# Softplus of the scans' preparation: summed in PSUM by identity matmuls instead of on VectorE

## The chip, the cores and the metric

The kernel runs on one core of a Trainium2 chip. The metric is the device time of one execution in microseconds (us). The engines are PE (TensorE), DVE (VectorE), ACT (ScalarE), POOL (GpSimd) and SP (SyncE, which only issues transfers).

## The reference, cut to what matters

The input is (8, 56, 56, 128) in f32: 8 images of 3136 pixels. Layers 0, 2 and 3 are deformable convolutions (each output pixel gathers 36 points, with bilinear weights, followed by a small MLP). Layer 1 is a two-dimensional state-space layer: over each image run four scans (rows, columns, both reversed) of 256 channels with 16 states each.

```python
x_dbl = jnp.einsum('bkdl,kcd->bkcl', xs, x_proj_w)
dts, Bsm, Csm = jnp.split(x_dbl, [R, R + N], axis=2)
dt = jnp.einsum('bkrl,kdr->bkdl', dts, dt_projs_w)
dt = jax.nn.softplus(dt + dt_projs_b[None, :, :, None])
...
def step(h, t):
    dt_t, u_t, B_t, C_t = t
    h = h * jnp.exp(dt_t[..., None] * A) + (dt_t * u_t)[..., None] * B_t[:, :, None, :]
    y = jnp.einsum('bkdn,bkn->bkd', h, C_t)
    return (h, y)
```

The change touches the line with `softplus` and the product `dt_t * u_t` behind it.

## The kernel before, in words

**Stages.** The deformable layers make 24 stages (3 layers x 8 images), in the order of `stage_order` (line 53), numbered 0 to 23; stage 20 is layer 2 of image 6, stage 21 layer 3 of image 6, stages 22 and 23 are layers 2 and 3 of image 7. A stage writes its projected image as a table to HBM, computes indices and weights in groups of four tiles of 128 pixels ("pr", DVE line 1724 writes the indices), and gathers. The gathers are indirect DMAs that POOL issues one by one (line 909). Twelve of them make a "third" of a tile, in one of five slots `d_g`. DVE multiplies a third by its weights (line 1523, "weigh"), PE sums it into PSUM by identity matmuls (line 1197, "sum"), which frees the slot for POOL (semaphore `accq`).

**Scans.** The state-space layer of an image runs beside the gathers of other images. It has 28 pieces (4 directions x 7 chunks of 448 pixels) of 16 states each, so 448 scan steps per image and 3584 in all. A step is: PE spreads B and C into banks `l_pb` and `l_pc` (line 1152), DVE multiplies dt*u by B (line 1497), ACT makes exp(dt*A) for both channel halves (line 961), DVE scans half 0 at once (line 1476) and half 1 in two parts (lines 1479 and 1482), multiplies by C (line 1503), ACT saves the carry (line 940), and PE adds the product to `l_acc` (line 1183).

**The preparation of a piece ("h", 224 times, nine parts 0 to 8)** runs one piece ahead. Part 0 projects into bank `r[1]` (`d_pr1`, called r1 here). Parts 1 and 2 put dt's projection for one channel half each into r1, from where ACT takes |x| into `e` (line 991) and relu(x) into `dtu` (line 994), which frees r1. Then, all on SBUF tiles of 128 x 896: exp(-|x|) on ACT (line 1000), u = 1 + e on DVE (1546), the rounding error (u - 1) - e on DVE (1549), relu minus that error on DVE (1553), ln u on ACT (1003), the sum dt on DVE (1557), and dt*u by the pixels on DVE (1561 for rows, 1563 for columns).

**What sets the order.** `Planner` puts scan ticks and stage work into one list; `takes_r1` tells it which scan items use bank r1, which the stages' own fetches ("ax"), tables ("at"), convolutions ("ac") and indices ("pr") share. The uses of a bank are numbered in that list's order. `schedule` looks for the pace, the number of scan ticks per third. `interleave` then makes each engine's own fixed queue out of lanes. All engines run their queues in order.

## Time and profile before

| | us |
|---|---|
| median of 3 runs | 28853.25 (28846.84 to 28859.32) |
| the profiled execution: device time | 28895.68 |
| the profiled execution: span, first to last instruction | 28893.9 |
| busy: PE / DVE / POOL / ACT | 22353.6 / 22852.5 / 21557.8 / 12154.5 |
| mean granted TensorE clock | 0.866 of 2.4 GHz |

A span is counted between the first and last recorded instruction. "Busy" leaves out the issuing and waiting of an engine's sequencer. The idle time named with a group is that of the engine just before its instructions, with what ended it; "issue" is time in which the engine waited for nothing that the profile shows.

### The profile page before, as it was taken

Reading aid. Unit: us, or ns where it says so; the run is one execution under the profiler, and the core shown is the slowest. Engines: PE = TensorE matmul, PEld = TensorE weight load, DVE = VectorE, ACT = ScalarE, POOL = GpSimd, SP = SyncE. Lnnn points to the kernel's source line nnn. Section 1 sums busy time; section 2 is a strip of 40 time slices with the busy share of each in tenths; the row PEclk is TensorE's granted clock in tenths of the full one; section 3 lists DMA queues with packets and bytes.
Section 4 is the critical chain, followed back from the end, with each engine's and each line's share of the span. In section 5 each row is a group of like instructions: output and inputs, shape, how many; then the busy total and the mean of one; then the engine's idle time right before and its main releaser. Section 6 shows DMA issues by size and latency. Waiting matters only on the chain.

```text
span 28893.9 us, 291528 instructions
## 1 busy us (share of the span) xinstructions
PE 22353.6 (77%) x94224; PEld 14447.1 (50%) x94224; DVE 22852.5 (79%) x36206; ACT 12154.5 (42%) x21719; POOL 21557.8 (75%) x21172
## 2 busy tenths in 40 slices
PE   6588788787887888877888788778878787777544
PEld 4455455454554555545545455445545454445443
DVE  2399988999699979998799969997899969995221
ACT  1254445444444445444444444444444444443100
POOL 6777777777777777777777777777777777576767
PEclk7798899898998999888998889889988898888666
DMA  3222132221322222212222132212222222112221
GB/s 79 69 59 69 54 77 65 59 69 54 79 66 56 68 69 64 69 54 67 71 65 69 54 78 60 62 56 75 66 62 63 56 76 58 47 53 73 65 57 53
DMA packets 2410696, 1854.82 MB, mean 64 GB/s; under 512 B 1686547, under 2 KB 2045509, under 8 KB 2409165
## 3 DMA queue, kind: packets, MB, share of 16 engines
q0 software_dynamic: 677376, 1388.62, 17.1%
q1 hardware_dynamic: 1731788, 447.55, 6.9%
q8 instruction: 746, 12.22, 0.2%
q14 instruction: 786, 6.43, 0.1%
HBM read 1569.35 MB, written 265.21 MB: 63 GB/s over the span
## 4 chain that ended last, share of the span: by engine, by line
POOL 63%; issue 21%; PE 7%; DVE 6%; ACT 1%; DMA 1%; SPq 1%; DVEq 0%; POOLq 0%; ACTq 0%
POOL d_g L909 63%; PE d_p L1197 2%; DVE l_wk L1476 1%; DVE l_wk L1497 1%; DVE l_wk L1503 1%; PE l_acc L1183 1%; PE d_pr L1347 1%; DVE d_g L1523 1%; DVE l_wk L1479 1%; PE l_pc L1312 0%; SPq L805 0%; DMA l_wk<-mid 0%; PE d_pr L1336 0%; PE d_pr L1335 0%; DMA d_g<-table,d_idx 0%
## 5 line engine op out<-in xcount | busy, mean ns | idle before, releaser
L909 POOL DMA_INDIRECT d_g<-table,d_idx x21168 | 21557.6, 1018 | 7300.2 <-issue 6436.2
L1197 PE MATMUL d_p<-d_g,c_ident 128*128 128x128 f32 x43200 | 6734.4, 327 | 2711.1 <-DVE d_g L1523 2709.5
L1197 PEld LDWEIGHTS d_p<-d_g,c_ident 128*128 128x128 f32 x43200 | 6503.2, 240 | 3408.7 <-DVE d_g L1523 2926.5
L1183 PE MATMUL l_acc<-l_wk,c_ident 128*128 128x448 f32 x14336 | 6597.3, 585 | 114.2 <-DVE l_yx L1461 102.1
L961 ACT ACTIVATE l_pm<-l_wk,l_a 128x448 f32<-128x448 f32 x3584 | 2282.6, 637 | 8608.2 <-DVE l_wk L1476 8585.1
L1503 DVE TENSOR_TENSOR l_wk<-l_wk,l_pc 128x896 f32<-128x896 f32 x3584 | 3857.3, 1076 | 493.2 <-PE l_pc L1152 254.2
L1497 DVE TENSOR_TENSOR l_wk<-l_wk,l_pb 128x896 f32<-128x896 f32 x3584 | 3836.5, 1070 | 85.9 <-PE l_pb L1152 83.4
L1183 PEld LDWEIGHTS l_acc<-l_wk,c_ident 128*128 128x128 f32 x14336 | 2921.8, 205 | 1827.8 <-issue 1725.8
L1476 DVE TENSOR_TENSOR_SCAN l_wk<-l_pm,l_carry,l_wk 128x448 f32<-128x448 f32 x3072 | 3522.9, 1147 | 1.0
L1523 DVE TENSOR_TENSOR d_g<-d_g,d_wt 128x512 f32<-128x512 f32 (+1 forms) x1385 | 880.4, 690 | 2559.7 <-DMA d_g<-table,d_idx 2559.5
L1523 DVE TENSOR_TENSOR d_g<-d_g,l_pm 128x1536 f32<-128x1536 f32 (+1 forms) x1309 | 2279.8, 1742 | 429.2 <-DMA d_g<-table,d_idx 379.6
L1152 PE MATMUL l_pc<-l_spl,c_sel 96*128 96x448 bf16 x3584 | 1356.0, 378 | 1501.1 <-DVE l_wk L1503 1494.7
L1482 DVE TENSOR_TENSOR_SCAN l_wk<-l_wk 128x224 f32<-128x224 f32 x3584 | 2448.3, 683 | 1.5
L961 ACT ACTIVATE l_wk<-l_wk,l_a 128x448 f32<-128x448 f32 x3584 | 2339.5, 653 | 2.9 <-DVE l_wk L1557 0.9
L1152 PE MATMUL l_pb<-l_spl,c_sel 96*128 96x448 bf16 x3584 | 1334.9, 372 | 1191.9 <-DVE l_wk L1497 1184.5
L1479 DVE TENSOR_TENSOR_SCAN l_wk<-l_wk,l_carry 128x224 f32<-128x224 f32 x3072 | 2051.0, 668 | 1.0
L1152 PEld LDWEIGHTS l_pb<-l_spl,c_sel 96*128 96x128 bf16 x3584 | 354.6, 99 | 2684.6 <-DVE l_wk L1497 2267.7
L1152 PEld LDWEIGHTS l_pc<-l_spl,c_sel 96*128 96x128 bf16 x3584 | 361.7, 101 | 2387.5 <-DVE l_wk L1503 2130.7
L961 ACT ACT_TABLE_LOAD x1132 | 1452.4, 1283 | 126.9 <-DVE l_wk L1476 107.9
L1347 PE MATMUL d_pr<-d_xt,d_diag 128*128 128x448 f32 x3024 | 1270.6, 563 | 23.7 <-ACT d_xt L1076 17.8
L1112 ACT ACTIVATE d_ys<-d_p 128x256 f32<-128x256 f32 x288 | 109.0, 378 | 2434.8 <-PE d_p L1197 2430.2
L1770 DVE BATCH_NORM_STATS2 d_bs<-d_pr 128x6 f32<-128x128 f32 (+1 forms) x1200 | 297.7, 289 | 887.0 <-PE d_pr L1403 492.0
(180 smaller groups left out, 24483.5 us busy)
## 6 DMA issues: line engine op xcount, KB each, us to landing
d_g<-table,d_idx POOLq DMA_INDIRECT x21168
table<-d_pst SPq DMA_DIRECT2D x2376, 64.0 KB
hd<-d_hst SPq DMA_DIRECT2D x168, 224.0 KB
d_htc<-hd SPq DMA_DIRECT2D x144, 256.0 KB
d_xin<-mid SPq DMA_DIRECT2D x112, 224.0 KB, 2.9
mid<-d_xo SPq DMA_DIRECT2D x192, 128.0 KB
d_xres<-mid SPq DMA_DIRECT2D x192, 128.0 KB
d_xin<-in_x SPq DMA_DIRECT2D x56, 224.0 KB, 3.2
```

Of the source, the lines that this page charges most:

```text
L909: e.indirect_dma_start(out=m.g[Q % SLOTS][:, j, :], out_offset=None, in_=m.table[k % 2], in_offset=bass.IndirectOffsetOnAxis(ap=m.idx[G % ...
L961: e.activation(m.dA0 if h == 0 else m.dA1[x % 3], m.dt[P % 2][:, h, :], ACT.Exp, scale=m.aa[:, kd, h, n:n + 1]).then_inc(s[f"dA{h}"], 1)
L1152: return e.matmul(bank[:, 0:448], m.sel[:, row + n:row + n + 1].to_broadcast([96, 128]), m.spl[P % 2][:, :], start=True, stop=True)
L1183: ins = e.matmul(m.acc[:, h, 0:448], m.ident[:, :], m.hb[x % 4][:, h, :], start=(n == 0), stop=(n == 15))
L1197: ins = e.matmul(m.p0[:, t % 2 * 128:t % 2 * 128 + 32 * w], m.ident[:, :], m.g[Q % SLOTS][:, w * p:w * p + w, 32 * r:32 * r + 32], start=( ...
L1347: ins = e.matmul(m.r[1][:, 0:448], m.diag[:, j, :], m.xt[:, 8 * c + dy:8 * c + dy + 8, dx:dx + 56], start=(j == 0), stop=(j == 8))
L1476: e.tensor_tensor_scan(hb[:, 0, way], m.dA0[:, way], hb[:, 0, way], ini, ALU.mult, ALU.add).then_inc(s["sh"], 1)
L1479: e.tensor_tensor_scan(hb[:, 1, one], dA1[:, one], hb[:, 1, one], ini, ALU.mult, ALU.add).then_inc(s["s1h"], 1)
L1482: e.tensor_tensor_scan(hb[:, 1, two], dA1[:, two], hb[:, 1, two], hb[:, 1, mid:mid + 1], ALU.mult, ALU.add).then_inc(s["sh"], 1)
L1497: e.tensor_tensor(m.hb[x % 4][:, :, :], m.dtu[P % 2][:, :, :], bc(m.pb[:, 0:448], 1, 2), ALU.mult).then_inc(s["f_pb"], 1)
L1503: e.tensor_tensor(m.hb[x % 4][:, :, :], m.hb[x % 4][:, :, :], bc(m.pc[:, 0:448], 1, 2), ALU.mult).then_inc(s["f_pc"], 1)
L1523: ins = e.tensor_tensor(g, g, wt, ALU.mult)
```

## The change

The softplus is computed from the same terms, elsewhere. Per channel half: after |x| and relu(x), ACT writes exp(-|x|) back into bank r1 (which is therefore not free yet) and copies -u = -(1 + e) from there into `dt`. DVE forms the rounding correction from -u (SBUF) and e (PSUM) into `e` in one instruction of 448 columns, and frees the bank. ACT takes ln over both halves at once, as before. PE adds relu, ln and the correction in r1 by three identity matmuls; ACT copies the sum to `dt`; DVE multiplies the sum, from PSUM, by the pixels and frees the bank. Five of nine parts use r1 now.

```diff
 def takes_r1(item):
-    return item[0] == "c" or item[0] == "h" and item[3] < 3
+    return item[0] == "c" or item[0] == "h" and item[3] < 5
...
# ACT
-                e.activation(m.dtu[P % 2][:, h, :], m.r[1][:, 0:448], ACT.Relu, bias=bia).then_inc(s["f_r1"], 1)
+                e.activation(m.dtu[P % 2][:, h, :], m.r[1][:, 0:448], ACT.Relu, bias=bia).then_inc(s["ab"], 1)
+                e.wait_ge(s["ab"], 4 * P + 2 * h + 2)
+                e.activation(m.r[1][:, 0:448], m.e[:, h, :], ACT.Exp, scale=-1.0).then_inc(s["ex"], 1)
+                e.wait_ge(s["ex"], 2 * P + h + 1)
+                e.activation(m.dt[P % 2][:, h, :], m.r[1][:, 0:448], ACT.Copy, scale=-1.0, bias=-1.0).then_inc(s["uu"], 1)
...
-                e.activation(m.e[:, :, :], m.e[:, :, :], ACT.Exp, scale=-1.0).then_inc(s["ex"], 1)
-            elif st == 6:
-                e.wait_ge(s["qq"], P + 1)
-                e.activation(m.dt[P % 2][:, :, :], m.dt[P % 2][:, :, :], ACT.Ln).then_inc(s["ln"], 1)
+                e.wait_ge(s["f_r1"], J.free("h1", P))
+                e.activation(m.dt[P % 2][:, :, :], m.dt[P % 2][:, :, :], ACT.Ln, scale=-1.0).then_inc(s["ln"], 1)
+            elif st in (4, 5):
+                h = st - 4
+                e.wait_ge(s["p_r1"], J.full(f"s{h}", P))
+                e.activation(m.dt[P % 2][:, h, :], m.r[1][:, 0:448], ACT.Copy).then_inc(s["d1"], 1)
...
# PE
+            elif st in (3, 4):
+                h = st - 3
+                e.wait_ge(s["ln"], P + 1)
+                e.wait_ge(s["f_r1"], J.use[f"s{h}", P])
+                e.matmul(m.r[1][:, 0:448], m.ident[:, :], m.dtu[P % 2][:, h, :], start=True, stop=False)
+                e.matmul(m.r[1][:, 0:448], m.ident[:, :], m.dt[P % 2][:, h, :], start=False, stop=False)
+                e.matmul(m.r[1][:, 0:448], m.ident[:, :], m.e[:, h, :], start=False, stop=True).then_inc(s["p_r1"], 1)
...
# DVE
-                e.tensor_scalar(dt[:, :, :], m.e[:, :, :], 1.0, None, ALU.add).then_inc(s["uu"], 1)
...
-                e.scalar_tensor_tensor(m.e[:, :, :], dt[:, :, :], -1.0, m.e[:, :, :], ALU.add,
-                                       ALU.subtract).then_inc(s["qq"], 1)
...
-                e.tensor_tensor(dtu[:, :, :], dtu[:, :, :], m.e[:, :, :], ALU.subtract).then_inc(s["s1"], 1)
...
-                e.tensor_tensor(dt[:, :, :], dtu[:, :, :], dt[:, :, :], ALU.add).then_inc(s["d1"], 1)
...
-                    e.tensor_tensor(dtu[:, :, :], dt[:, :, :], m.pixels(m.xb[:, :, :], kd, c), ALU.mult).then_inc(s["d2"], 1)
...
+            elif st in (3, 4):
+                h = st - 3
+                e.wait_ge(s["uu"], 2 * P + h + 1)
+                e.scalar_tensor_tensor(m.e[:, h, :], dt[:, h, :], 1.0, m.r[1][:, 0:448], ALU.add,
+                                       ALU.add).then_inc(s["f_r1"], 1)
+            elif st in (5, 6):
+                h = st - 5
+                e.wait_ge(s["d1"], 2 * P + h + 1)
+                z, to = m.r[1][:, 0:448], dtu[:, h, :]
+                if kd % 2:
+                    z, to = (x.rearrange("p (x y) -> p x y", y=56) for x in (z, to))
+                e.tensor_tensor(to, z, m.pixels(m.xb[:, h, :], kd, c), ALU.mult).then_inc(s["f_r1"], 1)
```

In the kernel after, DVE's correction is line 1559 and its product line 1567; the scan's lines 1476, 1479, 1482, 1497, 1503 and 1523 are 1490, 1493, 1496, 1511, 1517 and 1537; PE's spreads, product sums and gather sums (1152, 1183, 1197) are 1159, 1190 and 1204; the identity matmuls are lines 1234 to 1236. The order calls scans SCALAR_TENSOR_TENSOR.

DVE, preparation of piece 51 (image 1, columns reversed), before. `l_wk0` is e, `l_wk4` is dtu, `l_wk2` is dt:

```order
L1546 TENSOR_SCALAR l_wk2<-l_wk0 128x896
L1482 SCALAR_TENSOR_TENSOR l_wk9<-l_wk5,l_wk9 128x224
L1549 SCALAR_TENSOR_TENSOR l_wk0<-l_wk2,l_wk0 128x896
L1503 TENSOR_TENSOR l_wk8<-l_wk8,l_pc 128x896
L1553 TENSOR_TENSOR l_wk4<-l_wk4,l_wk0 128x896
L1696 TENSOR_TENSOR d_cc<-d_pr1,c_hw 128x288
L1697 TENSOR_REDUCE d_mx<-d_pr1 128x16
L1557 TENSOR_TENSOR l_wk2<-l_wk4,l_wk2 128x896
L1700 TENSOR_TENSOR d_ee<-d_pr1,d_mx 128x144
L1702 TENSOR_SCALAR d_cc<-d_cc 128x288
L1563 TENSOR_TENSOR l_wk4<-l_wk2,l_xb 128x896
```

DVE, the same piece in the changed kernel, from its second correction to its first product (`d_pr1` is bank r1):

```order
L1559 SCALAR_TENSOR_TENSOR l_wk0<-l_wk2,d_pr1 128x448
L1490 SCALAR_TENSOR_TENSOR l_wk10<-l_pm,l_carry,l_wk10 128x448
L1493 SCALAR_TENSOR_TENSOR l_wk10<-l_wk5,l_carry,l_wk10 128x224
L1511 TENSOR_TENSOR l_wk11<-l_wk3,l_pb 128x896
L1496 SCALAR_TENSOR_TENSOR l_wk10<-l_wk5,l_wk10 128x224
L1517 TENSOR_TENSOR l_wk9<-l_wk9,l_pc 128x896
L1490 SCALAR_TENSOR_TENSOR l_wk11<-l_pm,l_carry,l_wk11 128x448
L1493 SCALAR_TENSOR_TENSOR l_wk11<-l_wk6,l_carry,l_wk11 128x224
L1511 TENSOR_TENSOR l_wk8<-l_wk3,l_pb 128x896
L1496 SCALAR_TENSOR_TENSOR l_wk11<-l_wk6,l_wk11 128x224
L1517 TENSOR_TENSOR l_wk10<-l_wk10,l_pc 128x896
L1567 TENSOR_TENSOR l_wk4<-d_pr1,l_xb 128x448
```

The chain stood within one scan step; now it is spread over several, and the instructions left are half as wide and read the bank.

PE, the first sum of the same piece in the changed kernel:

```order
L1159 MATMUL l_pb<-l_spl0,c_sel 128x448
L1234 MATMUL d_pr1<-l_wk4,c_ident 128x448
L1235 MATMUL d_pr1<-l_wk2,c_ident 128x448
L1236 MATMUL d_pr1<-l_wk0,c_ident 128x448
L1159 MATMUL l_pc<-l_spl0,c_sel 128x448
L1190 MATMUL l_acc<-l_wk9,c_ident 128x448 x2
```

The three matmuls stand between the spread of B and the spread of C; before, nothing of the softplus was in PE's queue.

Counted over the whole queues: ACT has 3193 table loads before and 3215 now; copies of weights to PSUM (line 968), each of which lets a third be weighed in one instruction instead of three, are 1309 before and 1227 now. On DVE, between the last weighing of a stage and the last part of the next one's first index group stand 50 scan steps before at the change from stage 20 to 21, and 39 now; at the other changes that part stands ahead of the last weighing or at most one step behind it, before and now. By the end of stage 20 DVE's queue has 3386 of the 3584 steps before and 3441 now. An image's scans had ended and the next one's not begun at the change from stage 16 to 17 before (image 5), and now at those from 5 to 6 (image 1) and 13 to 14 (image 4).

## Rows read from the trace of the kernel before

**Rows 1.** The page: busy time by engine, and POOL's group of gathers
```profile
PE 22353.6 (77%) x94224; PEld 14447.1 (50%) x94224; DVE 22852.5 (79%) x36206; ACT 12154.5 (42%) x21719; POOL 21557.8 (75%) x21172
...
L909 POOL DMA_INDIRECT d_g<-table,d_idx x21168 | 21557.6, 1018 | 7300.2 <-issue 6436.2 <-DVE d_idx L1724 504.7 <-PE d_p L1197 270.4
```
**Rows 2.** The waits of POOL: us in total, times, longest
```profile
POOL d_g L909 <- DVE d_idx L1724: 504.7, 4, 259.5
POOL d_g L909 <- PE d_p L1197: 270.4, 43, 34.4
```
**Rows 3.** Line 909 by window: length, busy (instructions), clock, DMA share, GB/s
```profile
1262.00:25060.00 23798.00, 18126.81 (x17640) 0.90 0.24 65
26549.00:28894.00 2345.00, 1683.06 (x1764) 0.64 0.21 59
```
**Rows 4.** Timeline, 6633 to 6640 us, DVE and POOL: start, length
```profile
6633.34 1.08 DVE L1503 TENSOR_TENSOR l_wk<-l_wk,l_pc 128x896 f32<-128x896 f32 x1
...
6636.14 1.08 DVE L1557 TENSOR_TENSOR l_wk<-l_wk 128x896 f32<-128x896 f32 x1
...
6637.57 1.82 DVE L1563 TENSOR_TENSOR l_wk<-l_wk,l_xb 128x896 f32<-128x896 f32 x1
...
6633.51 0.95 POOL L909 DMA_INDIRECT d_g<-table,d_idx  x1 [0.30 <-issue]
6634.77 1.47 POOL L909 DMA_INDIRECT d_g<-table,d_idx  x1 [0.30 <-issue]
6636.54 1.49 POOL L909 DMA_INDIRECT d_g<-table,d_idx  x1 [0.30 <-issue]
6638.34 1.87 POOL L909 DMA_INDIRECT d_g<-table,d_idx  x1 [0.30 <-issue]
```
**Rows 5.** Groups by line and form, DVE: count, busy us, mean ns, idle before
```profile
L1557 DVE TENSOR_TENSOR l_wk<-l_wk 128x896 f32<-128x896 f32 x224 | 242.7, 1084 | 55.6 <-ACT l_wk L1003 47.3 <-issue 7.7
L1553 DVE TENSOR_TENSOR l_wk<-l_wk 128x896 f32<-128x896 f32 x224 | 242.4, 1082 | 0.2
L1549 DVE SCALAR_TENSOR_TENSOR l_wk<-l_wk 128x896 f32<-128x896 f32 x224 | 241.3, 1077 | 0.3
L1563 DVE TENSOR_TENSOR l_wk<-l_wk,l_xb 128x896 f32<-128x896 f32 x112 | 203.9, 1820 | 0.0
...
L1546 DVE TENSOR_SCALAR l_wk<-l_wk 128x896 f32<-128x896 f32 x224 | 142.7, 637 | 72.1 <-ACT l_wk L1000 71.9
...
L1561 DVE TENSOR_TENSOR l_wk<-l_wk,l_xb 128x896 f32<-128x896 f32 x112 | 121.2, 1082 | 0.1
...
L1456 DVE SCALAR_TENSOR_TENSOR l_yx<-l_xb,l_ds,l_acc 128x448 f32<-128x448 f32 x112 | 71.0, 676 | 2.1 <-PE l_acc L1183 2.1
```
**Rows 6.** Timeline of POOL over one scan step, 3001 to 3006 us
```profile
3001.77 0.94 POOL L909 DMA_INDIRECT d_g<-table,d_idx  x1 [0.31 <-issue]
3003.02 1.06 POOL L909 DMA_INDIRECT d_g<-table,d_idx  x1 [0.30 <-issue]
3004.39 1.27 POOL L909 DMA_INDIRECT d_g<-table,d_idx  x1 [0.30 <-issue]
```
**Rows 7.** The waits of DVE from 1262 to 25060 us
```profile
DVE d_g L1523 <- DMA d_g<-table,d_idx: 863.1, 357, 16.3
DVE l_wk L1503 <- PE l_pc L1152: 233.2, 272, 6.1
```
**Rows 8.** Groups by line and form, PE and ACT, and DVE's weighing from SBUF
```profile
L1183 PE MATMUL l_acc<-l_wk,c_ident 128*128 128x448 f32 x14336 | 6597.3, 585 | 114.2 <-DVE l_yx L1461 102.1 <-DVE l_yx L1456 11.7
...
L961 ACT ACTIVATE l_pm<-l_wk,l_a 128x448 f32<-128x448 f32 x3584 | 2282.6, 637 | 8608.2 <-DVE l_wk L1476 8585.1 <-issue 4.8
...
L1523 DVE TENSOR_TENSOR d_g<-d_g,d_wt 128x512 f32<-128x512 f32 x1369 | 875.0, 693 | 2559.7 <-DMA d_g<-table,d_idx 2559.5
```
**Rows 9.** The waits of POOL from 20000 to 20330 us
```profile
POOL d_g L909 <- DVE d_idx L1724: 48.3, 1, 48.3
POOL d_g L909 <- PE d_p L1197: 37.0, 2, 33.9
```

More of the change, by code:

```diff
@@ L386, in bank_uses @@
         return [("r1", ("cv", item[1], item[2], item[3]))]
-    if kind == "h" and item[3] < 3:
+    if kind == "h" and item[3] < 5:
         _, i, j, m = item
-        return [("r1", (("hx", "h0", "h1")[m], 28 * i + j))]
+        return [("r1", (("hx", "h0", "h1", "s0", "s1")[m], 28 * i + j))]
     if kind == "sB":
@@ L949, in scalar_program @@
                 if n == 0:
-                    e.wait_ge(s["d1"], P + 1)
+                    e.wait_ge(s["d1"], 2 * P + 2)
                 if h == 0 and q == 0:
@@ L986, in scalar_program @@
                 e.wait_ge(s["p_r1"], J.full(f"h{h}", P))
-                if h == 0 and j:
-                    e.wait_ge(s["s1"], P)
+                if h == 0 and P:
+                    e.wait_ge(s["p_r1"], J.full("s1", P - 1))
                 if h == 0 and j == 0 and i:
@@ L993, in scalar_program @@
                     e.wait_ge(s["f_pb"], J.free("B", 16 * (P - 2) + 15))
-                e.activation(m.dtu[P % 2][:, h, :], m.r[1][:, 0:448], ACT.Relu, bias=bia).then_inc(s["f_r1"], 1)
+                    for b in range(2):
+                        e.wait_ge(s[f"dA{b}"], 16 * (P - 1))
+                e.activation(m.dtu[P % 2][:, h, :], m.r[1][:, 0:448], ACT.Relu, bias=bia).then_inc(s["ab"], 1)
[3 more added lines that the diff above has]
+                e.activation(m.dt[P % 2][:, h, :], m.r[1][:, 0:448], ACT.Copy, scale=-1.0, bias=-1.0).then_inc(s["uu"], 1)
                 if h == 1:
@@ L998, in scalar_program @@
             elif st == 3:
-                e.wait_ge(s["ab"], 2 * P + 2)
-                e.activation(m.e[:, :, :], m.e[:, :, :], ACT.Exp, scale=-1.0).then_inc(s["ex"], 1)
-            elif st == 6:
-                e.wait_ge(s["qq"], P + 1)
-                e.activation(m.dt[P % 2][:, :, :], m.dt[P % 2][:, :, :], ACT.Ln).then_inc(s["ln"], 1)
+                e.wait_ge(s["f_r1"], J.free("h1", P))
[4 more added lines that the diff above has]
+                e.activation(m.dt[P % 2][:, h, :], m.r[1][:, 0:448], ACT.Copy).then_inc(s["d1"], 1)
         elif kind == "c" and item[4] == 2:
@@ L1488, in vector_program @@
             if n == 0:
-                e.wait_ge(s["d2"], P + 1)
+                e.wait_ge(s["f_r1"], J.free("s1", P))
             if sig == -1:
@@ L1541, in vector_program @@
                 e.tensor_tensor(m.spl[P % 2][64:96, :], m.bcd[0:32, :], m.bcm[:, :], ALU.subtract).then_inc(s["lo"], 1)
-            elif st == 4:
-                if P >= 2:
-                    e.wait_ge(s["sh"], 32 * (P - 1))
-                e.wait_ge(s["ex"], P + 1)
-                e.tensor_scalar(dt[:, :, :], m.e[:, :, :], 1.0, None, ALU.add).then_inc(s["uu"], 1)
-            elif st == 5:
-                e.wait_ge(s["uu"], P + 1)
-                e.scalar_tensor_tensor(m.e[:, :, :], dt[:, :, :], -1.0, m.e[:, :, :], ALU.add,
-                                       ALU.subtract).then_inc(s["qq"], 1)
-            elif st == 6:
-                e.wait_ge(s["qq"], P + 1)
-                e.tensor_tensor(dtu[:, :, :], dtu[:, :, :], m.e[:, :, :], ALU.subtract).then_inc(s["s1"], 1)
-            elif st == 7:
-                e.wait_ge(s["s1"], P + 1)
-                e.wait_ge(s["ln"], P + 1)
-                e.tensor_tensor(dt[:, :, :], dtu[:, :, :], dt[:, :, :], ALU.add).then_inc(s["d1"], 1)
-            elif st == 8:
-                e.wait_ge(s["d1"], P + 1)
-                if kd % 2 == 0:
-                    e.tensor_tensor(dtu[:, :, :], dt[:, :, :], m.pixels(m.xb[:, :, :], kd, c), ALU.mult).then_inc(s["d2"], 1)
-                else:
-                    e.tensor_tensor(dtu[:, :, :].rearrange("p h (x y) -> p h x y", y=56),
-                                    dt[:, :, :].rearrange("p h (x y) -> p h x y", y=56), m.pixels(m.xb[:, :, :], kd, c),
-                                    ALU.mult).then_inc(s["d2"], 1)
+            elif st in (3, 4):
[10 more added lines that the diff above has]
+                e.tensor_tensor(to, z, m.pixels(m.xb[:, h, :], kd, c), ALU.mult).then_inc(s["f_r1"], 1)
         elif kind == "p":
@@ L1798 @@
          "weighed accq ysa ytp yta idx wtr w0 pv py exd bst agg sqd x1r xor gbr dgr bsq bnr "
-         "wps dA0 dA1 s1h sh ca accd d1 d2 hd0 md m2 lo ab ex uu qq s1 ln pag psq xir brd lag lsq xmr gsq gt gb tg").split()
+         "wps dA0 dA1 s1h sh ca accd d1 hd0 md m2 lo ab ex uu ln pag psq xir brd lag lsq xmr gsq gt gb tg").split()
 def program(nc, a, out, n_img=8, layers=(0, 1, 2, 3)):
```

## The prediction

> **What bounds the kernel now.** I read the page first. By busy time no engine is full: DVE 79%, PE 77%, POOL 75%, ACT 42% [rows 1]. But line 909, POOL's one line, is one indirect DMA of a deformable-convolution gather, 21168 of them, 1.018 us each on average, and each is followed by 0.304 us of "issue" (6436.2 us in all). 21168 x (1.018 + 0.304) is 27.98 ms of a span of 28.89 ms: POOL is the bound, hidden in a busy share of 75%.
>
> Next the waits of POOL: beyond "issue" it sat idle for 504.7 us in front of indices (4 times, 259.5 us at most) and for 270.4 us in front of a free gather slot [rows 2]. So the time is (number of gathers) x (length of one) plus some 0.8 ms, and only what shortens a gather or removes such an idle stretch can shorten the kernel.
>
> Then the length of a gather by stretch. Over the scans (1262 to 25060 us) it is 18126.81/17640 = 1.028 us, in the last two stages, which have no scans beside them, 1683.06/1764 = 0.954 us [rows 3]. Something in the scans holds gathers. The timeline shows what [rows 4]: the undisturbed gather takes 0.94 us. The one that begins at 6633.51, under line 1503 (one operand in PSUM), takes 0.95. The next three meet lines 1553, 1557 and 1563 (two operands in SBUF) and take 1.47, 1.49 and 1.87, and each ends 0.82 us behind the end of that DVE instruction: 6637.57 + 1.82 + 0.82 = 6640.21 = 6638.34 + 1.87. A DVE instruction that reads two SBUF operands stops a gather 0.12 to 0.2 us after its start until DVE is done. The Trainium skill names these kinds (GPSIMD Engine Reference, Specifications: the SBUF interfaces are shared with VectorE, in contention for instructions in a 2-port mode or with two SBUF inputs), but gives no price.
>
> Last, DVE's waits in the scans: 863.1 us were spent waiting for landed gathers, so DVE follows POOL and has that much in hand [rows 7].
>
> **The change, part by part.** Everything occurs once per piece, 4 x 7 x 8 = 224 times.
>
> 1. *Gather relief.* Lines 1546, 1549, 1553, 1557 and 1561/1563 go; all have SBUF operands only. In their place stand two SCALAR_TENSOR_TENSOR and two TENSOR_TENSOR of 448 columns with one operand in PSUM. By the gather under line 1503, those hold nothing. What the old ones cost: I went through all 21168 gathers and took those whose point 0.19 us after the start lies inside one of the six lines. They are 849, and over 0.941 us each they sum to 432 us, 1.93 us per piece; the sample has 0.53 + 0.55 + 0.93 = 2.01 [rows 4]. Lower bound: shared out by busy time alone. The excess in the scans is 17640 x (1.028 - 0.941) = 1535 us; the six lines are busy for 142.7 + 241.3 + 242.4 + 242.7 + 121.2 + 203.9 = 1194 us of DVE's 22852 [rows 1, 5], of which perhaps a third reads two SBUF operands, so some 1535 x 1194/7617 = 240 us. A long instruction holds more than its share, since more gathers meet it and each waits longer, so I take **-432**, and keep 240 for the range.
>
> 2. *Given back.* The scan halves (lines 1479, 1482) hold gathers too: in a cycle of 1.24 + 1.36 + 1.57 = 4.17 us the three gathers take 0.94, 1.06 and 1.27 us, 0.45 us over [rows 6]. DVE time that comes free is filled by such cycles. Freed per piece: 1194.2/224 = 5.33 us less the new work. Line 1456 (448 columns, PSUM operand) takes 0.676; half of 1561 is 0.54, half of 1563 (transposed pixels) 0.91, mean 0.73; 2 x 0.676 + 2 x 0.73 = 2.81 us [rows 5]. 2.5 us freed x 0.45/4.17 x 224 = **+60**. DVE's busy time falls by 560 us, off the path.
>
> 3. *Weights from SBUF.* The order moves 82 thirds (1309 to 1227 copies by line 968) from the PSUM form of the weighing to three instructions of two SBUF operands each, 246 in all, each 0.693 us long [rows 8]. A scan half of that length holds 0.12 or 0.33 us where it meets a gather, or nothing; at 0.15, **+37** (0 to 80).
>
> 4. *PE.* Two groups of three identity matmuls of 448 columns, 1344 in all, each two instructions of 585 ns [rows 8]: +1572 us busy, from 77 to 83%. One group holds PE's queue for 6 x 0.585 = 3.5 us, and the spreads of B and C (lines 1159) and the sums stand behind it. DVE lets a bank go about 3.5 us before it needs it again, so a group now and then makes line 1517 wait, as it does now for 233.2 us over 1554 sums of similar length [rows 7]; a quarter of that more, 60 us, paid from DVE's 863. On the path: **0**.
>
> 5. *ACT.* Two Copy more per half, and the exponential in halves to PSUM: about 4 x 0.6 + 0.3 = 2.7 us per piece by line 961's 0.637 [rows 8], 600 us in all on an engine at 42%; table loads stay (3193 and 3215 in the order). Queued behind them are the exponentials of the scan, one cycle ahead, and the carry copies. On the path: **0**.
>
> 6. *Bank r1.* The softplus keeps it for five uses instead of three, so the stages' fetches, tables and indices get fewer openings. The order shows where this ends. Between the last weighing of stage 20 and the indices of stage 21 DVE's queue has 39 scan steps where it had 50. Those 50 are the 259.5 us of [rows 2], 5.2 us a step: 11 x 5.2 = **-57**. But two image ends (images 1 and 4) now fall on a change of stage, with no scan step on either side, where before one did (image 5). That one costs POOL 33.9 + 48.3 us, part of the sums above [rows 9]: **+82**.
>
> Sum: -432 + 60 + 37 - 57 + 82 = **-310 us**. The profiled execution took 28895.7 us (span 28893.9) and would take 28586; the median of the runs is 28853, 42 us or 0.15% lower, so I forecast 28853 - 310 = **28543, say 28540 us**.
>
> DVE must still be ahead: 863 in hand + 560 saved - 60 - 286 (55 scan steps more done by the end of stage 20, at 5.2) - 432 (POOL's time shrinks) is about 645 us, 2.9 us per piece.
>
> The Trainium skill speaks of one removed instruction in another way (Vector Engine (DVE) Microarchitecture Reference, Points that are easy to get wrong: a scalar_tensor_tensor with two non-bf16 SBUF sources runs at half throughput). The trace differs: line 1549, of that kind, takes 1077 ns and the plain line 1553 1082 [rows 5]. By the rule DVE would save another 240 us, off the path; the row decides.
>
> **The rivals.**
> - *The softplus chain makes DVE late (slower).* DVE's queue is in order, and per piece it now waits four times on ACT: twice for u, twice for the copied sum, which stands behind a PE group. In the old chain it waited once each on exponential and logarithm. If these waits and those behind the PE groups pass 2.9 us per piece, the gather slots fill and POOL waits at line 909 for PE's sums. With both groups' 3.5 us exposed, 7 us per piece, it costs 224 x 4.1 = 920 us: 29460 us. It is slower than before from 2.9 + 310/224 = 4.3 us per piece on. For it: PE is already busy for 77% and DVE nearly full. Against: softplus runs some ten scan steps before it is needed, the queues are interleaved, and the present PE waits are small. 13%.
> - *The relief is mostly given back.* Gathers meet other instructions instead; only the proportional share goes. -240 + 60 + 37 + 25 = -118: 28735 us. For it: gather and scan cycle lock into each other [rows 6]. 15%.
> - *Bank r1 is too short.* Indices of other stages come late, each time some 22 steps of 5.2 us, 114 us; two such: -310 + 230 = -80, 28773 us. For it: three uses became five. Against: at all other changes of stage the indices stand ahead of the first weighing as before. 10%.
> - *The whole DVE time of the six lines comes back to POOL*, 1194 instead of 432: 27780 us. So the Trainium skill's rule on shared interfaces would read if contention meant exclusion throughout. Against: undisturbed gathers of 0.94 lie beside these instructions, and DVE would bind first. 2%.
>
> **How the numbers follow.** My forecast has 60%, from 28260 (nothing lost at image ends, all of item 1) to 28700. What a measurement can tell from no change is about 0.2%, 58 us. Most of the second and third rival are faster than that (they centre at -0.3%), a part is within it. The low end is 28853 - 432 - 57 - 100 (stalls at images' ends gone) = 28260. The high end takes in the second and third rival, 28850. Beyond it stays what is slower. Faster 0.77, within 0.2% 0.10, slower 0.13.
>
> **What would show it.** Line 909's mean falls from 1018 to about 1000 ns with the gap at 0.304; gathers under the new lines 1559 and 1567 stay at 0.94; the wait at stage 21 is near 200 us; DVE's busy time is lower by some 530 us and its waits for gathers stay above 300 us; PE is near 83%. It is wrong if line 909 waits for PE's sums for far more than 270 us, if waits on indices grow beyond 505 us, or if the mean of a gather stays.

## The result and the profile after

The changed kernel took **28323.9 us** in the median of 4 runs (28318.9 to 28348.7); the kernel before, on the same chip, 28850.0 us (28842.0 to 28859.3). The ratio is 0.9818, 95% interval 0.9806 to 0.983: 526 us faster, where 310 were forecast. The profiled execution took 28326.8 us, its span is 28325.0 us, the mean granted clock 0.887 (before 0.866).

The page of the changed kernel: busy time by engine, the head of the chain that ended last, and the gathers.

```profile
PE 22717.0 (80%) x96912; PEld 14592.4 (52%) x96912; DVE 22312.8 (79%) x36148; ACT 12657.4 (45%) x22779; POOL 21096.9 (74%) x21172
...
POOL 35%; DVE 23%; PE 18%; issue 17%; ACT 5%; DMA 1%; SPq 1%; DVEq 0%; POOLq 0%; ACTq 0%
...
L909 POOL DMA_INDIRECT d_g<-table,d_idx x21168 | 21096.7, 997 | 7193.3 <-issue 6431.6
```

Beside [rows 1]: the same 21168 gathers take 460.9 us less in all, 997 ns each in place of 1018, and the "issue" behind them is what it was (6431.6, was 6436.2). The rest of the 569 us between the two spans, 108 us, is idle time of POOL. Its waits, as in [rows 2]:

```profile
POOL d_g L909 <- DVE d_idx L1726: 376.7, 4, 218.7
POOL d_g L909 <- PE d_p L1204: 297.9, 59, 35.9
POOL d_g L909 <- DMA table<-d_pst: 87.1, 1, 87.1
```

Waits for indices fell by 128 us, waits for a free slot rose by 27. The gathers by window, in the columns of [rows 3] (the scans, then the two last stages):

```profile
1260.00:24617.00 23357.00, 17697.83 (x17640) 0.92 0.24 66
25984.00:28325.00 2341.00, 1682.03 (x1764) 0.64 0.21 59
```

The last stages, where the change puts nothing, are equal (1683.06 and 1682.03). Beside the scans a gather takes 1003 ns in place of 1028. The timeline shows how, start and length first as in [rows 4]; line 1567 is the new product, with one operand in PSUM:

```profile
2936.81 0.94 POOL L909 DMA_INDIRECT d_g<-table,d_idx  x1 [0.30 <-issue]
2936.91 0.62 DVE L1567 TENSOR_TENSOR l_wk<-d_pr,l_xb 128x448 f32<-128x448 f32 x1 [2.41 <-ACT l_wk L1010]
...
2941.68 0.66 DVE L1493 TENSOR_TENSOR_SCAN l_wk<-l_wk,l_carry 128x224 f32<-128x224 f32 x1
...
2941.80 1.29 POOL L909 DMA_INDIRECT d_g<-table,d_idx  x1 [0.30 <-issue]
2942.26 0.60 DVE L1567 TENSOR_TENSOR l_wk<-d_pr,l_xb 128x448 f32<-128x448 f32 x1
```

The gather at 2936.81 meets line 1567 and takes 0.94. The one at 2941.80 begins inside a scan half (line 1493, SBUF operands only), which ends at 2942.34, and ends at 2943.09, 0.75 us behind it. That line 1567 begins at 2942.26 makes no difference. The same held in all 434 gathers whose point 0.19 us after the start lies inside one of the two new lines: 944 ns on average.

A gather is put down here to the DVE instruction that runs 0.19 us after the gather's start; where two overlap there, to the earlier one. Another choice among them moves a row by up to some 15 us. With this count (that of the prediction's item 1) the time over 0.941 us per gather can be shared out by the instruction under that point. The middle column is a second profiled run of the kernel before (experiment 5, span 28857.4, gathers 21507.4 us), which is nearer to that kernel's median:

| us over 0.941 each | before, recorded | before, again | changed |
|---|---|---|---|
| the six lines of the old softplus, or the two new ones | 432 | 431 | 1 |
| scan halves (1479 and 1482, now 1493 and 1496) | 769 | 761 | 760 |
| weighing from SBUF (1523, now 1537) | 120 | 99 | 132 |
| all others | 318 | 297 | 285 |
| sum | 1639 | 1588 | 1178 |

The groups of the changed kernel that answer to [rows 5, 8]:

```profile
L1559 DVE SCALAR_TENSOR_TENSOR l_wk<-l_wk,d_pr 128x448 f32<-128x448 f32 x448 | 272.5, 608 | 122.1 <-ACT l_wk L1000 120.7
L1567 DVE TENSOR_TENSOR l_wk<-d_pr,l_xb 128x448 f32<-128x448 f32 x448 | 354.8, 792 | 147.1 <-ACT l_wk L1010 146.3
```

```profile
L1234 PE MATMUL d_pr<-l_wk,c_ident 128*128 128x448 f32 x896 | 462.6, 600 | 89.8 <-ACT l_wk L1006 68.8 <-DVE l_wk L1567 20.7
L1235 PE MATMUL d_pr<-l_wk,c_ident 128*128 128x448 f32 x896 | 440.4, 575 | 0.0
L1236 PE MATMUL d_pr<-l_wk,c_ident 128*128 128x448 f32 x896 | 430.0, 563 | 0.0
L1190 PE MATMUL l_acc<-l_wk,c_ident 128*128 128x448 f32 x14336 | 6424.6, 572 | 101.8 <-DVE l_yx L1475 86.9 <-DVE l_yx L1470 14.6
```

DVE's new work is 627 us where the old was 1194. PE's is 1333 us, yet PE is busy for only 363 us more: with the mean granted clock at 0.887 in place of 0.866, the sums of line 1190 alone, unchanged in number, take 173 us less than in [rows 8]. DVE's waits from 1260 to 24617 us, as in [rows 7]:

```profile
DVE d_g L1537 <- DMA d_g<-table,d_idx: 608.0, 174, 24.1
DVE l_wk L1517 <- ACT l_carry L940: 256.2, 244, 9.8
DVE l_wk L1517 <- PE l_pc L1159: 179.5, 171, 9.8
DVE l_wk L1567 <- ACT l_wk L1010: 134.3, 74, 8.0
DVE l_wk L1559 <- ACT l_wk L1000: 114.9, 92, 7.3
```

DVE still waits for gathers, for 608 us (it was 863.1), so POOL still leads. The new chain costs DVE 249 us of waiting on ACT (the two last lines), 1.1 us per piece. The old chain's two waits on ACT cost 116 us over the scans (70.4 at line 1546, 45.4 at line 1557), so the rise is 133 us, 0.6 us per piece.

### The profile page after: what moved, and what is told of

It is laid out like the page before. It is cut to its first block, busy times and chain, and to the rows that moved or that the text cites. A ratio compares the mean times of both kernels' runs of the same rounds, so it can differ in the third digit from the quotient of the medians.

```text
span 28325.0 us, 298054 instructions
## 1 busy us (share of the span) xinstructions
PE 22717.0 (80%) x96912; PEld 14592.4 (52%) x96912; DVE 22312.8 (79%) x36148; ACT 12657.4 (45%) x22779; POOL 21096.9 (74%) x21172
## 4 chain that ended last, share of the span: by engine, by line
POOL 35%; DVE 23%; PE 18%; issue 17%; ACT 5%; DMA 1%; SPq 1%; DVEq 0%; POOLq 0%; ACTq 0%
POOL d_g L909 35%; PE d_p L1204 6%; DVE l_wk L1490 5%; DVE l_wk L1511 4%; DVE l_wk L1517 4%; DVE d_g L1537 3%; PE l_acc L1190 3%; DVE l_wk L1493 3%; PE d_pr L1361 1%; DVE l_wk L1496 1%; PE l_pb L1159 1%; SPq L805 1%; PE d_pr L1415 1%; ACT L961 1%; PE d_pr L1220 1%
## 5 line engine op out<-in xcount | busy, mean ns | idle before, releaser
L909 POOL DMA_INDIRECT d_g<-table,d_idx x21168 | 21096.7, 997 | 7193.3 <-issue 6431.6
L1204 PE MATMUL d_p<-d_g,c_ident 128*128 128x128 f32 x43200 | 6419.9, 317 | 2366.9 <-DVE d_g L1537 2364.7
L1204 PEld LDWEIGHTS d_p<-d_g,c_ident 128*128 128x128 f32 x43200 | 6224.5, 231 | 2970.5 <-DVE d_g L1537 2536.8
L1190 PE MATMUL l_acc<-l_wk,c_ident 128*128 128x448 f32 x14336 | 6424.6, 572 | 101.8 <-DVE l_yx L1475 86.9
L1190 PEld LDWEIGHTS l_acc<-l_wk,c_ident 128*128 128x128 f32 x14336 | 2863.2, 201 | 1802.0 <-issue 1705.3
L1537 DVE TENSOR_TENSOR d_g<-d_g,d_wt 128x512 f32<-128x512 f32 (+1 forms) x1633 | 1039.4, 690 | 2663.8 <-DMA d_g<-table,d_idx 2663.6
L1537 DVE TENSOR_TENSOR d_g<-d_g,l_pm 128x1536 f32<-128x1536 f32 x1227 | 2124.6, 1732 | 163.2 <-DMA d_g<-table,d_idx 121.8
```

Source lines behind the costliest of these rows:

```text
L909: e.indirect_dma_start(out=m.g[Q % SLOTS][:, j, :], out_offset=None, in_=m.table[k % 2], in_offset=bass.IndirectOffsetOnAxis(ap=m.idx[G % ...
L1190: ins = e.matmul(m.acc[:, h, 0:448], m.ident[:, :], m.hb[x % 4][:, h, :], start=(n == 0), stop=(n == 15))
L1204: ins = e.matmul(m.p0[:, t % 2 * 128:t % 2 * 128 + 32 * w], m.ident[:, :], m.g[Q % SLOTS][:, w * p:w * p + w, 32 * r:32 * r + 32], start=( ...
L1537: ins = e.tensor_tensor(g, g, wt, ALU.mult)
```

## The experiments

**Theory A**: a gather is held only while a DVE instruction with all its operands in SBUF runs; DVE's and PE's own time is off the path, and what remains is how many scan steps the order leaves at a change of stage. **Theory B**: the gain is DVE's freed time (560 us, about the gain itself), and the shorter gathers are a by-product. **Theory C**: it is the new order of the queues. An edit that adds or removes an instruction also shifts the order that `interleave` makes, so experiments 2, 4 and 5 do not have the changed kernel's order to the last instruction; the two kernels of a pair in experiment 2 have the same one, and experiment 3 has the changed kernel's.

The runs fell on chips of two sorts. The kernel before took 28850, 28860 and 28884 us in three groups of runs and 35187 and 35377 us in two others; each experiment is compared with the kernel before on its own chip.

### 1. The changed kernel again, on a slower chip

> The changed kernel itself, as the measure for the three runs beside it. Both theories: 28324 us, ratio 0.982, a gather of 997 ns on average.

Measured: 35615.1 us against 35186.5 for the kernel before, ratio 1.0126 (1.0095 to 1.0157). **On this chip the change makes the kernel slower.** Neither 28324 us nor 0.982 nor the mean gather of 997 ns (it is 985) came out. The page and POOL's waits:

```profile
PE 24461.0 (69%) x96912; PEld 15284.8 (43%) x96912; DVE 22379.8 (63%) x36148; ACT 12670.0 (36%) x22779; POOL 20846.8 (59%) x21172
...
L909 POOL DMA_INDIRECT d_g<-table,d_idx x21168 | 20846.6, 985 | 14709.4 <-issue 6070.5
...
POOL d_g L909 <- PE d_p L1204: 5562.2, 553, 57.4
POOL d_g L909 <- remote: 1979.3, 702, 10.0
```

DVE and ACT are busy for the same time as on the first chip, and POOL's gathers take 250 us less in all. But POOL, which waited there for 298 us for PE's sums, waits 5562 us, so gathers no longer set the time ("remote" is a wait whose releaser the profile does not name). PE is busy for 24461 us in place of 22717, at a mean granted clock of 0.802 in place of 0.887. Whether the lower clock is a cause of its late instructions or follows from its idle time, no run tells. The timeline shows one place:

```profile
2077.34 0.27 PE L1204 MATMUL d_p<-d_g,c_ident 128*128 128x128 f32 x1 [1.47 <-issue]
...
2078.74 0.29 PEld L1204 LDWEIGHTS d_p<-d_g,c_ident 128*128 128x128 f32 x1 [2.61 <-issue]
...
2080.14 0.37 PE L1204 MATMUL d_p<-d_g,c_ident 128*128 128x128 f32 x1 [2.54 <-issue]
...
2081.54 0.29 PEld L1204 LDWEIGHTS d_p<-d_g,c_ident 128*128 128x128 f32 x1 [2.51 <-issue]
...
2082.93 0.37 PE L1204 MATMUL d_p<-d_g,c_ident 128*128 128x128 f32 x1 [2.42 <-issue]
```

In the middle of one sum of 24 matmuls, with nothing to wait for, PE starts an instruction every 1.40 us, by turns on its two queues. I counted stretches of over 0.25 us in which both of PE's queues stand idle before an instruction that has no wait: 1874 in this trace, 1358 us in all, and not one in any trace of the faster chips, of either kernel (none among some 6400 us of PE's idle time in the kernel before, run again). Such holes explain 1.4 of the 7.3 ms between this chip's time and the first's directly. Idle time before instructions that do wait grew as well, from about 5500 to 9400 us, and how much of that is a late instruction and how much a late operand the trace doesn't tell. What makes them late was not found. The kernel before has no trace on a slower chip, so why it loses less there than the changed kernel is not shown by a trace either; experiment 4 bears on it.

### 2. The pair: one DVE multiply more, with its second operand in PSUM or in SBUF

Both kernels add one instruction of 448 columns to each half, 448 in all, and are the same in the order of every engine. The PSUM one:

```
             elif st in (3, 4):
                 h = st - 3
                 e.wait_ge(s["uu"], 2 * P + h + 1)
+                e.tensor_tensor(m.wk[6][:, 1, :].rearrange("p (a b) -> p a b", b=8),
+                                dt[:, h, :].rearrange("p (b a) -> p a b", b=8),
+                                m.r[1][:, 0:448].rearrange("p (a b) -> p a b", b=8), ALU.mult)
                 e.scalar_tensor_tensor(m.e[:, h, :], dt[:, h, :], 1.0, m.r[1][:, 0:448], ALU.add,
```

In the SBUF one `dt[:, h, :]`, of the same size, stands in the added lines for `m.r[1][:, 0:448]`. The result goes to a scratch tile, and only the first operand is read in transposed steps.

On the first slower chip:

> The changed kernel with one more DVE multiplication of 448 columns per channel half (448 in all, result unused, dt read in transposed steps, some 0.9 us each), its second operand in PSUM. Theory A (the gain is that gathers are no longer held by DVE instructions with SBUF operands alone, DVE's time is off the path): DVE gets 400 us more work, which its 608 us of waits for gathers in the scans take up; the mean gather stays at 997 ns and the time within 28300 to 28400 us. Theory B (the gain is DVE's shorter busy time): 400 us longer, about 28720 us.

> The same additional multiplication, but with its second operand also in SBUF; DVE's time is the same. Theory A: each holds gathers, by the square of its length: lines of 0.68 us held 0.15 us each and the 1.82 us line 1.08 us each, so about 0.3 us each for 0.9 us, +110 to +160 us over the PSUM twin, and a mean gather of some 1003 ns. Theory B: the same time as the PSUM twin.

On the second:

> The changed kernel with one more VectorE multiply in each half of each softplus piece (448 of them), after the subtraction that is left; its second operand is the PSUM bank r1, its result goes to a scratch tile. It adds some 448 x 0.85 = 380 us of VectorE work. Theory A (a gather's issue is held only behind VectorE instructions whose operands all lie in SBUF; VectorE's own time lies off the path): the gathers' mean stays at 997 ns (+-3), the time rises by 0 to 60 us over the changed kernel's. Theory B (the gain came from VectorE's busy time, the gathers' shorter mean being a by-product): most of the 380 us come back, +200 us or more, gathers' mean unchanged. If this call lands on a chip where TensorE's instruction supply bounds (the changed kernel 1.2% slower than before there), both say little and the time stands by the added TensorE and VectorE waits.

> The twin of the kernel with the extra multiply on PSUM: the same instruction at the same place, but its second operand is a tile in SBUF. Theory A: 448 instructions of some 0.7 us in which a gather's issue is held again; gathers' mean 1003 to 1008 ns, 110 to 160 us more gather time than its PSUM twin, and the kernel 90 to 160 us slower than the twin. Theory B: equal to the twin within 30 us.

On a faster chip:

> The third go of the pair, for its time on a chip of the first sort (kernel before at 28.85 ms). The changed kernel with 448 more VectorE multiplies whose second operand is PSUM r1, some 0.85 us each (380 us of VectorE busy on the two slower chips). Theory A (gathers are held only behind VectorE instructions with all operands in SBUF, and VectorE's own time is off the path): gathers' mean 997 ns +-3, the time 0 to 60 us above 28324, so 0.982 to 0.984 of the kernel before. Theory B (VectorE's busy time sets the time): +200 us or more, 0.989 or more. On a slow chip: 1.021 to 1.023 as twice before.

> Its twin with the second operand in SBUF. On the two slower chips 281 gathers began under this multiply and took 1324 ns each, 107 us over the undisturbed ones. Theory A on a chip of the first sort: 90 to 160 us slower than the PSUM twin, gathers' mean +4 to +7 ns over the twin's. Theory B: equal to the twin within 30 us. On a slow chip: equal to the twin within 0.3%, since gathers do not set the time there.

Measured:

| | kernel before, us | PSUM | SBUF | SBUF less PSUM, us |
|---|---|---|---|---|
| slower chip 1 | 35186.5 | 1.0225 (1.02 to 1.0249) | 1.0231 (1.02 to 1.0262) | -29 |
| slower chip 2 | 35376.6 | 1.0212 (1.0185 to 1.0239) | 1.0265 (1.0239 to 1.0292) | +118 |
| faster chip | 28884.0 | 0.9852 (0.9836 to 0.9869) | 0.9875 (0.9858 to 0.9891) | +59 |

The traces of the faster chip at the same place in both, PSUM first (DVE and POOL, start and length):

```profile
5117.57 0.96 DVE L1559 TENSOR_TENSOR l_wk<-l_wk,d_pr 128x448 f32<-128x448 f32 x1
...
5117.91 0.94 POOL L909 DMA_INDIRECT d_g<-table,d_idx  x1 [0.30 <-issue]
...
5118.97 0.68 DVE L1493 TENSOR_TENSOR_SCAN l_wk<-l_wk,l_carry 128x224 f32<-128x224 f32 x1
...
5119.16 1.24 POOL L909 DMA_INDIRECT d_g<-table,d_idx  x1 [0.30 <-issue]
```

```profile
5120.16 0.96 DVE L1559 TENSOR_TENSOR l_wk<-l_wk 128x448 f32<-128x448 f32 x1
...
5120.50 1.38 POOL L909 DMA_INDIRECT d_g<-table,d_idx  x1 [0.30 <-issue]
...
5121.56 0.68 DVE L1493 TENSOR_TENSOR_SCAN l_wk<-l_wk,l_carry 128x224 f32<-128x224 f32 x1
...
5122.19 0.94 POOL L909 DMA_INDIRECT d_g<-table,d_idx  x1 [0.30 <-issue]
```

In both a gather begins 0.34 us behind the start of the same instruction, which takes the same 0.96 us. With a PSUM operand the gather takes 0.94, with SBUF operands 1.38, and ends 0.76 us behind the multiply. That is the mechanism with one operand changed and nothing else. In all, 290 gathers meet the PSUM multiply (mean 945 ns, 1 us over 0.941 each) and 291 the SBUF one (1319 ns, 110 us over). The slower chips show the same in their traces: 275 gathers at 944 ns against 281 at 1324, and 263 at 944 against 270 at 1303.

The second half of the fences shows why the kernel doesn't pay these 110 us in full. The gather that wasn't held runs into the scan half behind it and takes 1.24; the one that was held comes out past it. Scan halves hold 790 us of gathers in the PSUM kernel and 765 in the SBUF one, weighing 141 and 133. The gathers' sum differs by 66 us:

```profile
L909 POOL DMA_INDIRECT d_g<-table,d_idx x21168 | 21140.3, 999 | 7280.8 <-issue 6432.4
```

```profile
L909 POOL DMA_INDIRECT d_g<-table,d_idx x21168 | 21206.7, 1002 | 7265.6 <-issue 6432.6
```

The time follows with 59 us. So A had sign and place right and the size too high: 90 to 160 us and 4 to 7 ns were expected, 59 us and 3 ns came. B's "within 30 us" fails: the slowest run with the PSUM operand (28462.0 us) is faster than the fastest with SBUF ones (28486.9).

The PSUM kernel was slower than the changed one by more than A's 60 us: 133 us by the medians, 99 by the ratios (0.9852 less 0.9818, of 28.9 ms), for 378 us of DVE's time. In the profiles it is 131 us: 44 in gathers and 87 in POOL's idle time. There the waits for indices are 130 us longer (506.5 in place of 376.7) and those for slots 44 shorter (253.9 in place of 297.9). Most of the 130 lies in one wait, here in the PSUM kernel (24000 to 25200 us):

```profile
POOL d_g L909 <- DVE d_idx L1729: 323.9, 1, 323.9
```

In the changed kernel it is 218.7. The number of times line 1517 (once per scan step, line 1503 in the kernel before) runs inside that wait tells what it is:

| | wait at stage 21, us | scan steps in it | us each |
|---|---|---|---|
| before | 259.5 | 50 | 5.2 |
| changed | 218.7 | 40 | 5.5 |
| changed, two terms (experiment 5) | 231.9 | 43 | 5.4 |
| pair, PSUM | 323.9 | 61 | 5.3 |
| pair, SBUF | 324.8 | 61 | 5.3 |

So what the added multiply cost beyond the gathers lies mainly where the order leaves scan steps in front of the indices, 61 of them in place of 40, and B, which wanted 200 us or more back, fails. On the slower chips it is otherwise: the pair on the first of them costs 377 and 348 us over the changed kernel (35992 and 35963 against 35615), nearly the whole 380 us of DVE's time. There too POOL's waits for indices grew, from 987 to 1279 us with the PSUM operand, so these 377 us do not speak for B alone. On that chip the kind of operand makes no difference to the time, as it should where gathers don't set it. The 118 us on the second lie in the range that A gave, but the runs of the two kernels overlap, and the mean gather is 982 and 989 ns where A expected 997 and 1003 to 1008; I leave them.

### 3. One operand of the last product moved back to SBUF

```
                 e.wait_ge(s["d1"], 2 * P + h + 1)
-                z, to = m.r[1][:, 0:448], dtu[:, h, :]
+                z, to = dt[:, h, :], dtu[:, h, :]
```

> One operand of the changed kernel moved back: the last product dt*u reads dt from its SBUF copy instead of from the bank, everything else and all waits as changed. Theory A: 448 instructions of 0.55 us (rows) and 0.91 us (columns) with SBUF operands alone hold 0.1 and 0.3 us each: +60 to +110 us against the changed kernel, mean gather 1000 to 1003 ns. Theory B (DVE's busy time) and theory C (the order and the stalls made the gain): no difference.

> The changed kernel with one operand of the last product (dt x u, 448 instructions) read from the SBUF copy of dt in place of PSUM r1: nothing is added, one operand moves. Theory A: VectorE busy falls some (0.79 to 0.65 us each, -60 us) but gathers are held behind these 448 instructions again: gathers' mean +3 to +6 ns, the time +60 to +110 us. Theory B: the time falls with VectorE's busy time, 0 to -60 us.

Measured, on the slower chips only: 1.0116 (1.0092 to 1.014) and 1.0136 (1.0106 to 1.0167), where the changed kernel had 1.0126 on the first (on the second it was not run). The gathers did what A says: 203 met the product on either chip, at 1326 and 1334 ns, 78 and 80 us over 0.941 each; in the changed kernel on the first slower chip as many met it, at 945 ns. The mean gather went from 985 to 989 and 990 ns; 1000 to 1003 was expected. The product took 803 ns with the SBUF operand and 795 with the PSUM one on the first slower chip, so no DVE time was saved. The kernel's time doesn't answer, since there POOL is not the bound. On a faster chip it wasn't tried.

### 4. The group of identity matmuls twice

```
                 e.wait_ge(s["f_r1"], J.use[f"s{h}", P])
+                e.matmul(m.r[1][:, 0:448], m.ident[:, :], m.dtu[P % 2][:, h, :], start=True, stop=False)
+                e.matmul(m.r[1][:, 0:448], m.ident[:, :], m.dt[P % 2][:, h, :], start=False, stop=False)
+                e.matmul(m.r[1][:, 0:448], m.ident[:, :], m.e[:, h, :], start=False, stop=True)
                 e.matmul(m.r[1][:, 0:448], m.ident[:, :], m.dtu[P % 2][:, h, :], start=True, stop=False)
```

> The changed kernel with the group of three identity matmuls that builds the softplus done twice into the same bank (the first group is overwritten): 3 x 448 more matmuls and weight loads on TensorE, and the bank is ready later. My forecast put TensorE's added work at nothing on the path. If that is right: within +40 us of the changed kernel. If TensorE's part is on the path (the scans then wait longer for its sums): +100 us or more, VectorE's waits for PE in the scans longer by as much. On a chip where TensorE's instruction supply bounds, +1% or more.

Measured, on the second slower chip: 37636.7 us, ratio 1.0644 (1.0614 to 1.0674), 0.052 or some 1.8 ms over the changed kernel's 1.0126, which was measured on the other slower chip. That is 0.68 us for each of the 2688 added matmuls, more than one takes (0.58 us on average in this run's trace, over both groups). POOL's waits for PE's sums, 5562 us in experiment 1:

```profile
POOL d_g L909 <- PE d_p L1204: 7782.7, 605, 59.7
```

On this chip PE's added work is on the path, as its own time or as a longer softplus chain; the run doesn't part the two. PE's busy time is only 975 us above that of experiment 1, so about half of the 1.8 ms is waiting. The order moved too: DVE has 97 weighings from SBUF more and 34 from PSUM less than in experiment 1. The price of 0.68 us is thus an upper figure for a matmul with all that came with it.

### 5. The third matmul left out, and the kernel before once more

```
                 e.matmul(m.r[1][:, 0:448], m.ident[:, :], m.dtu[P % 2][:, h, :], start=True, stop=False)
-                e.matmul(m.r[1][:, 0:448], m.ident[:, :], m.dt[P % 2][:, h, :], start=False, stop=False)
-                e.matmul(m.r[1][:, 0:448], m.ident[:, :], m.e[:, h, :], start=False, stop=True).then_inc(s["p_r1"], 1)
+                e.matmul(m.r[1][:, 0:448], m.ident[:, :], m.dt[P % 2][:, h, :], start=False, stop=True).then_inc(s["p_r1"], 1)
```

> The changed kernel without the third identity matmul (the rounding correction is computed as before but not added: 896 matmul records and 896 weight loads less). Where TensorE is off the path, as my forecast had it (term 4 at nothing): within 40 us of the changed kernel, ratio to the kernel before 0.980 to 0.984. On a chip like the two on which all experiments so far ran (kernel before at 35.2 ms), if TensorE sets the time there: doubling the group cost 1815 us for 2688 matmuls, 0.675 us each, so 896 less should give back about 605 us, ratio near 0.996; if TensorE is not what costs there but the length of the softplus chain, less than 200 us.

> The kernel before, unchanged, for its trace on the chip of this call. If that chip is of the slower sort: 94224 matmuls with some 1800 idle gaps on TensorE's two queues over 0.25 us that nothing is waited for in (none in the recorded trace of before), GpSimd's waits for TensorE's sums some 4500 to 5000 us (5562 in the changed kernel there) and gathers at 1003 to 1008 ns. If it is of the first sort: 28.85 ms and none of these.

Measured, on a faster chip: 28297.4 us against 28860.0, ratio 0.9804 (0.9788 to 0.982); the kernel before against itself 1.0. A third of PE's added work is worth nothing that can be told: the intervals of 0.9804 and 0.9818 overlap. The page of the second profile of the kernel before:

```profile
PE 22313.9 (77%) x94224; PEld 14397.5 (50%) x94224; DVE 22849.0 (79%) x36206; ACT 12154.4 (42%) x21719; POOL 21507.6 (75%) x21172
...
L909 POOL DMA_INDIRECT d_g<-table,d_idx x21168 | 21507.4, 1016 | 7313.9 <-issue 6434.8
```

Its span is 36 us shorter than the recorded one's and its gathers take 50 us less: the recorded execution of the kernel before was a long one, and its gathers had been held for longer.

Against this profile the gain is accounted for: gathers -411, waits for indices -128 (504.6 to 376.7), waits for slots +12 (286.4 to 297.9), "issue", the table's wait and the end -5, together -532 us, which is the difference of the spans (28857.4 and 28325.0).

Theory C was not tried by itself: no run had the new order with the old softplus. What speaks on it is the account above and the table of experiment 2: 411 of the 532 us lie in the length of the gathers, which the order does not explain, since 434 gathers still met the new lines and were not held; the 116 us less of stalls are the order's part. So C is right for about a fifth of the gain.

## Why the prediction was right, and where it was wrong

The sign, the cause and the range held. 526 us were measured, 310 forecast. Between the spans of the second profile of the kernel before and of the changed one it is 532, so 222 us are to be placed.

- **Item 1, gather relief, -432**: 431 us (before again) became 1. Line 1546 reads a single operand, from SBUF, and held gathers too (95 of them took 1183 ns in the second profile), so "two SBUF operands" was said too narrowly: what the removed lines share is that no operand lay in PSUM. The lower bound of 240, taken by busy time, was of no use: the table above shows scan halves holding 761 us in 4.8 ms of DVE's time, the six lines 431 in 1.2 ms.
- **Item 2, given back, +60**: wrong in its reasoning. Scan halves hold 760 us in the changed kernel, 761 before. The freed time is not "filled by such cycles": their number is fixed, the same 7168 halves run in either kernel. The freed time lets them run sooner.
- **Item 3, weights from SBUF, +37**: +12 against the recorded profile, +33 against the second; 250 of these instructions were added.
- **Item 4, PE, 0**: shown for a third of the work (experiment 5), on the faster chips. The other two thirds were not taken out by any run there. PE's busy share is 80%, not 83; the sum had taken each matmul at the 585 ns of a mean granted clock of 0.866, and the changed kernel ran at 0.887, with 572 ns for the same line. The forecast that line 1517 waits 60 us longer for PE failed: 179.5 in place of 233.2. On a slower chip the term is worth more than the whole gain.
- **Item 5, ACT, 0**: +503 us busy (600 forecast) and 133 us more of DVE's waits on ACT in the softplus (249 in place of 116), while its waits for gathers fell by 255.
- **Item 6, stage 21, -57**: -41. The price of 5.2 us per scan step held (5.5); 40 steps stood in the wait, one more than counted.
- **Item 6, the image ends, +82**: this is the step that failed. The order showed the ends of images 1 and 4 at a change of stage, and I gave each the 82 us that the end of image 5 cost [rows 9]. Neither cost a wait for indices. The changed kernel has 47 us of slot waits around the first of these ends (7000 to 7400 us) and no wait of note at the second:

```profile
POOL d_g L909 <- PE d_p L1204: 47.5, 3, 35.9
```

But a slot wait was no mark of an end that meets a change of stage: in the kernel before each of the eight images' ends has one, the longest of each between 9 and 34 us (28.8 us at 7405, for instance), so the 33.9 us should not have been counted for the coincidence. And the waits for the indices of stages 17 and 22, 48.3 us [rows 9] and 49.1 us (26300 to 26600 us), went away, but for one new wait of 10.0 us at 3578:

```profile
POOL d_g L909 <- DVE d_idx L1724: 49.1, 1, 49.1
```

Before, slot waits at an image's end lay at 20112 to 20163 us and the change of stage at 20261, with no scan step between; now they lie at 19459 to 19532 and the change at 19927, with 33 scan steps of the next image between. At stage 22 no scans are left, but the last image's end moved away from the change: it was 26434 to 26463 with the change at 26500, and is 25652 to 25689 with the change at 25984. That distance from an image's end decides the wait is read from these two places; no run tested it. In all, waits for indices and slots fell by 116 us (from 504.6 + 286.4 to 376.7 + 297.9) where the two parts of item 6 added 25. That is 141 of the 222; item 2 is 61 more, and the rest is item 3 and the instructions that I left aside. The term of 82 had taken one occurrence's price for a rule, without asking what DVE had to do between the end and the change.

Of the rivals, *the softplus chain makes DVE late* came nearest to an effect: DVE's waits on ACT in the new chain are 1.1 us per piece, 0.6 more than in the old one, against 2.9 in hand. DVE's reserve (608 us of waits for gathers) came out close to the 645 forecast. *Bank r1 is too short* did not come: the waits for indices fell from 505 to 377 us, and the only new one was 10.0 us. *The relief is mostly given back* is refuted for the change by the table, though experiment 2 shows its mechanism at work between neighbours: 110 us of holding cost 66. *The whole DVE time comes back* (27780) is refuted: of the 1194 us of these lines the gathers gave back 431. The rival that I did not have is the one that decides elsewhere: PE as the bound, on a chip where it gets its instructions late. There the change is 1.3% slower. By experiment 4's price of 0.68 us a matmul, the 2688 added ones would cost 1.8 ms and all the rest of the change would gain 1.4; that is an estimate from a price that holds more than the matmul itself, and its second half is not shown by any run.

## What to carry to other kernels

When one engine's issue loop sets the time, look past its "busy" to the length of one instruction by what runs beside it: the relief is worth at most what the removed neighbours held (411 us of 430 here; in experiment 2 a holding of 110 us cost 66), and an instruction that reads one operand from PSUM held nothing, at the same length. Stalls at changes of stage are worth (steps that the order leaves there) x (time of one step), counted in the new order and never carried over from another place. Measure on more than one chip before trading DVE or POOL work for PE instructions: the same two kernels stood 1.8% one way on one chip and 1.3% the other way on another.

## What was not expected of the hardware

- Two sorts of chip: 28.85 to 28.88 and 35.19 to 35.38 ms for the same program. DVE's and ACT's busy time and an undisturbed gather (0.94 us) were the same on both. PE's instructions came late, with 1669 to 1930 holes without a wait in a trace against none, up to 2.5 us long, and each took longer (624 ns for line 1190 against 572, granted clock 0.802 against 0.887). I found no cause.
- In the pair the place of one operand alone decided whether DVE held a gather: 945 ns beside a PSUM operand, 1319 beside SBUF ones, with the DVE instruction itself at 971 and 973 ns. One operand can be enough: line 1546, with a single one in SBUF, held its gathers to 1183 ns.
- A held gather ends 0.75 us behind a scan half, 0.76 behind the pair's multiply and 0.82 to 0.83 behind the six lines of the old softplus.
- Reading one operand in transposed steps (the pair's multiply reads dt so) went with 971 ns for a 448-column instruction, where line 1559, another operation with plain reads, takes 608.
- In the kernels with more matmuls each one was shorter: PE was busy for 77, 79 and 80% with 94224, 96016 (two terms) and 96912 of them, the granted clock was 0.866, 0.882 and 0.887, and the sums of line 1190 took 585 ns in the first kernel and 572 in the last.
